# Causal attention: four banks of PSUM for the scores and three for the products for the maxima, in place of three and four

## The reference, cut to what matters

```python
c_q = x @ W_dq
Q = (c_q @ W_uq).reshape(Bx, Sx, N_HEADS, D_K)
c_kv = x @ W_dkv
K = (c_kv @ W_uk).reshape(Bx, Sx, N_HEADS, D_K)
V = (c_kv @ W_uv).reshape(Bx, Sx, N_HEADS, D_K)
scores = jnp.einsum('bqhd,bkhd->bhqk', Q, K) / math.sqrt(D_K)
causal = jnp.tril(jnp.ones((Sx, Sx), dtype=bool))
scores = jnp.where(causal, scores, -jnp.inf)
attn = jax.nn.softmax(scores, axis=-1)
out = jnp.einsum('bhqk,bkhd->bqhd', attn, V).reshape(Bx, Sx, N_HEADS * D_K)
return out @ W_o
```

## Time and profile before

| | us |
|---|---|
| median of 3 runs | 1355.92 |
| lowest, highest | 1352.75, 1357.1 |
| the profiled execution | 1350.49 |
| its span, first to last instruction | 1348.8 |
| TensorE, VectorE, ScalarE, GpSimd busy | 1224.4, 1120.5, 923.6, 745.1 |

### The profile page before, as it was taken

One profiled execution on the slowest core, in us unless ns is written; L12 is line 12 of the kernel. 1 busy time (PEld: TensorE's weight loads), 2 busy tenths in 40 slices (PEclk: granted clock), 3 DMA queues, 4 the chain that ended last, 5 costly groups with the idle time before them and its releaser, 6 DMA issues. The chain is left out here.

```text
span 1348.8 us, 30203 instructions
## 1 busy us (share of the span) xinstructions
PE 1224.4 (91%) x10501; PEld 705.0 (52%) x10501; DVE 1120.5 (83%) x2928; ACT 923.6 (68%) x2463; POOL 745.1 (55%) x753
## 2 busy tenths in 40 slices
PE   4589999999999999888899999799899999997895
PEld 2323434434443443356566666565466666665663
DVE  5788998898999888689899999766599999997675
ACT  4516776777787677678888888433588888885344
POOL 1111212332331233478999999532699999997244
PEclk9859999999999999999999999899999999998998
DMA  4432121112112101011111111100112111111001
GB/s 106 130 107 75 45 59 46 61 51 64 39 39 58 46 15 35 26 40 41 34 30 34 33 33 33 41 0 1 24 32 48 33 33 33 31 27 25 1 17 47
DMA packets 35486, 56.46 MB, mean 42 GB/s; under 512 B 6898, under 2 KB 22652, under 8 KB 33020
## 3 DMA queue, kind: packets, MB, share of 16 engines
q1 hardware_dynamic: 34760, 54.39, 15.3%
q10 hardware_dynamic: 576, 0.15, 0.0%
HBM read 27.78 MB, written 8.39 MB: 27 GB/s over the span
## 5 line engine op out<-in xcount | busy, mean ns | idle before, releaser
L1128 ACT ACTIVATE a_prob<-a_psE 128x512 f32<-128x512 f32 (+1 forms) x608 | 303.0, 591 | 132.1 <-PE a_psE L741 130.6
L1527 DVE CUSTOM_DVE_ANT_0 a_psM<-a_psM,mask_q 128x384 f32<-128x384 f32 (+3 forms) x512 | 234.3, 521 | 32.2 <-PE a_psM L725 31.4
L1360 POOL TENSOR_SCALAR_AFFINE_SELECT a_prob<-a_prob 128x512 f32<-128x512 f32 x128 | 81.1, 641 | 310.0 <-ACT a_prob L1128 306.2
L741 PE MATMUL a_psE<-a_qs,a_ks 84*128 84x512 bf16 (+3 forms) x768 | 238.1, 333 | 12.9 <-ACT a_prob L1128 6.3
L725 PE MATMUL a_psM<-a_ks,a_qs 72*128 72x512 bf16 (+3 forms) x768 | 241.8, 343 | 7.3 <-PEq L106 3.2
L1419 POOL TENSOR_TENSOR w_rn<-w_ssm,mhalf 128x16 f32<-128x16 f32 x64 | 220.5, 3445 | 49.0 <-DVE w_ssm L1619 33.7
L1238 ACT ACTIVATE w_prob<-w_psS,w_bias 128x128 f32<-128x128 f32 x512 | 180.4, 378 | 21.1 <-DVE w_bias L1645 21.1
L1404 POOL TENSOR_TENSOR w_t<-w_raw,w_sin 128x256 f32<-128x256 f32 x252 | 176.6, 734 | 0.0
L1529 DVE TENSOR_REDUCE a_nm<-a_psM 128x1 f32<-128x512 f32 x256 | 158.7, 680 | 15.1 <-PE a_psM L725 13.8
L1409 POOL TENSOR_TENSOR w_rot<-w_t,w_t 128x1024 f32<-128x1024 f32 x63 | 148.7, 2360 | 8.7 <-issue 0.4
L741 PEld LDWEIGHTS a_psE<-a_qs,a_ks 84*128 84x128 bf16 x768 | 74.3, 98 | 148.3 <-ACT a_prob L1128 76.1
(11 more groups left out here) (189 smaller groups left out, 2383.7 us busy)
## 6 DMA issues: line engine op xcount, KB each, us to landing
a_qs<-q_parts SPq DMA_DIRECT2D x16, 576.0 KB
a_ks<-k_parts SPq DMA_DIRECT2D x16, 576.0 KB
q_parts<-p_parts SPq DMA_DIRECT2D x24, 128.0 KB
k_parts<-p_parts SPq DMA_DIRECT2D x24, 128.0 KB
w_vb__707<-w_v__691 SPq DMA_DIRECT2D x16, 128.0 KB, 2.2
w_vb__708<-w_v__691 SPq DMA_DIRECT2D x16, 128.0 KB, 2.3
w_vb__708<-w_v__692 SPq DMA_DIRECT2D x16, 128.0 KB, 2.2
w_vb__709<-w_v__692 SPq DMA_DIRECT2D x16, 128.0 KB, 2.4
```

The costliest lines, as they stand in the source:

```text
L741: mm = pe.matmul(psE[:, r % NRING, j % share * w:(j % share + 1) * w], ks[0:KROWS, g, j, kt * P:(kt + 1) * P], qs[0:KROWS, g, j, q0:q0 + w ...
L1128: act.activation(prob[G % NPROB][:, j - share + 1:j + 1, 0:w], psE[:, r % NRING, 0:share * w].rearrange("p (j n) -> p j n", j=share), ACT. ...
L1527: d = dve.tensor_tensor_reduce(scores, scores, sb["mask_q"][:, 512 - n:512], -1.0, -3.0 * NEG, ALU.add, ALU.min, low)
```

## The change

The rings are re-cut: `psM` has 3 banks, `psE` 4. A product for a maximum then waits for the reader of slot r - 3, a score for the reader of slot r - 4. Since `w_psV` now lies over the first bank of `psE`, from the last stage's first slots on (`E_NARROW`) the scores rotate through the other three banks, and `project_v(0)` waits until that first bank was read. The order of instructions on all five engines is the same as before, and so is the work of each.

```diff
+E_NARROW = E_SLOT["s", LAST_G - 11, 0] // 4 * 4
 def m_bank(r):
-    return r % 4 if r < M_TAIL else 2
+    return r % 3 if r < M_TAIL else 2
+def e_bank(r):
+    return r % 4 if r < E_NARROW else 1 + (r - E_NARROW) % 3
+def e_ring(r):
+    return 4 if r < E_NARROW else 3
...
-        NPROB, NRING, MRING = 5, 3, 4
+        NPROB, MRING = 5, 3
...
-            psE = banks.enter_context(nc.psum_tensor("a_psE", [P, NRING, 512], F32))
+            psE = banks.enter_context(nc.psum_tensor("a_psE", [P, 4, 512], F32))
...
-                    ge(pe, e_read, r - NRING + 1)
-                mm = pe.matmul(psE[:, r % NRING, j % share * w:(j % share + 1) * w], ks[0:KROWS, g, j, kt * P:(kt + 1) * P], qs[0:KROWS, g, j, q0:q0 + w],
+                    ge(pe, e_read, r - e_ring(r) + 1)
+                mm = pe.matmul(psE[:, e_bank(r), j % share * w:(j % share + 1) * w], ks[0:KROWS, g, j, kt * P:(kt + 1) * P], qs[0:KROWS, g, j, q0:q0 + w],
...
                 if G == LAST_G - 9:
+                    pe.wait_ge(e_read, E_NARROW - 3)
                     project_v(0)
```

More of the change, by code:

```diff
@@ L765, in turn_maxima @@
                 pe.wait_ge(nm_parts, 2 * s + half + 1)
-                ge(pe, e_read, r - NRING + 1)
+                ge(pe, e_read, r - e_ring(r) + 1)
                 for t in range(4):
                     i = 4 * half + t
-                    mm = pe.transpose(psEb[0:NM, r % NRING, t * P:(t + 1) * P], nmp[:, s % 2, i, :, :].rearrange("p j a -> p (j a)"), sb["ident_b"])
+                    mm = pe.transpose(psEb[0:NM, e_bank(r), t * P:(t + 1) * P], nmp[:, s % 2, i, :, :].rearrange("p j a -> p (j a)"), sb["ident_b"])
                 mm.then_inc(e_ready, 1)
@@ L791, in turn_o @@
                     r = E_SLOT["t", b, h]
-                    ge(pe, e_read, r - NRING + 1)
-                    out, done = psE[:, r % NRING, :], e_ready
+                    ge(pe, e_read, r - e_ring(r) + 1)
+                    out, done = psE[:, e_bank(r), :], e_ready
                 for t in range(4):
@@ L1127, in exps @@
                         act.wait_ge(e_ready, r + 1)
-                        act.activation(prob[G % NPROB][:, j - share + 1:j + 1, 0:w], psE[:, r % NRING, 0:share * w].rearrange("p (j n) -> p j n", j=share),
+                        act.activation(prob[G % NPROB][:, j - share + 1:j + 1, 0:w], psE[:, e_bank(r), 0:share * w].rearrange("p (j n) -> p j n", j=share),
                                        ACT.Exp, scale=SCALE0).then_inc(e_read, 1)
@@ L1134, in copy_maxima @@
                 ge(act, nm_in[half], 16 * (s - 1))
-                act.activation(nmT[:, s % 2, 512 * half:512 * half + 512], psEb[0:NM, r % NRING, 0:512], ACT.Copy).then_inc(e_read, 1)
+                act.activation(nmT[:, s % 2, 512 * half:512 * half + 512], psEb[0:NM, e_bank(r), 0:512], ACT.Copy).then_inc(e_read, 1)
             def copy_outputs(e, qc):
@@ L1154, in copy_turned @@
                 act.wait_ge(e_ready, r + 1)
-                act.activation(to, psE[:, r % NRING, :], ACT.Copy).then_inc(e_read, 1)
+                act.activation(to, psE[:, e_bank(r), :], ACT.Copy).then_inc(e_read, 1)
             def copy_projected(b, h):
```

## The result

| | before | after |
|---|---|---|
| median (4 runs each) | 1354.34 us | 1370.47 us |
| lowest, highest | 1350.84, 1357.1 | 1368.34, 1371.1 |
| the profiled execution | 1350.49 | 1370.99 |
| its span | 1348.8 | 1369.3 |

The ratio is 1.0118, with a 95% interval of 1.01 to 1.0135. The change costs 16 us by the medians and 20.5 us between the two profiled spans. The two figures fit together: the profiled execution of before lay 3.85 us under its median, that of after 0.5 us above.

What follows compares the result with a forecast made beforehand. VectorE was taken to bound the attention stages, its gaps all at bursts. Eleven stages at 1.78 us (19.6) plus 2.4 for four others gave 22 us, 1378 on the median, stated as 1377, range 1367 to 1387.

Steps and rivals of the forecast that it cites:

- VectorE is the engine to look at: Causal attention stages: VectorE works 25.92 of 28.40 us, ScalarE 20.89, so whatever lengthens VectorE's gaps lengthens the stage.
- The last slot of a segment waits for the reader of r - 3: TensorE's last load for VectorE before each burst waits for one later read; together 1.78 us a stage.
- C: Segment of a stage: turned output 0.43 us late, taken up by shorter waits for ScalarE; charged 0, bounds 0.43 and -0.1.
- B: Segment of a stage: last load moves from 307.65 to 308.24, nothing hides it; charged 0.60 us.
- D: Segment of a stage: turned output 0.53 us late, VectorE's gap of 1.80 us at the burst grows by 0.53.
- E: Segment of a stage: last load 0.65 us late, VectorE's gap of 0.54 us at the burst grows by that.
- A: Segment of a stage: last load 0.09 us late, behind work that VectorE still has; nothing charged.
- The fourth bank of `psE` gives back C's 0.43 and nothing else: Scores may start one exponential (0.50 us) sooner, but products for maxima stay pinned to VectorE; real gain in one segment only.
- A ring of three does not break VectorE's work inside segments: Rival expected the break: one slot a stage 0.5 us late, 14 us more, 1391; chance 0.14.
- The four stages charged at a third: The very first stage and three of some 31.20 us: a third of 1.78 us each, 4 x 0.6 = 2.4.
- The new wait and the narrow ring cost nothing: Last stage: scores keep three banks, and its values already wait for the exponentials asked for; no gain, no loss.
- the clock stays: Attention stages after the first keep 2.4 GHz; the rival, clock falling in two stages, up to 30 us, 1407, chance 0.02.

Runs made afterwards that it cites:

- m3e3: Kernel before with three banks of `psM` in place of four, `psE` kept at three, one bank left empty: 1375.29 us, ratio 1.0175.
- m2e4: Kernel after with two banks of `psM` in place of three, `psE` kept at four, one bank left empty: 1452.72 us, ratio 1.075.
- m5e2: Kernel before with five banks of `psM` in place of four and two of `psE` in place of three: 1414.33 us, ratio 1.0447.
- short_m4e3: Kernel before with VectorE reading only part of each product for its maximum, four banks of `psM`, three of `psE`: 1348.80 us, ratio 0.9975.
- one_m4e3: Kernel before with values of one group after nearly every group, taken a group later (`AV_LAG` 3): 1366.09 us, ratio 1.0093.

## Why the prediction was right, point by point

- **VectorE is the engine to look at, and TensorE's program is what feeds it.** Right: its busy time is unchanged, its waits grew by 20.1 us and the span by 20.5.
- **The last slot of a segment waits for the reader of r - 3.** Right, to 0.07 us or better, though in C two more slots come behind the output. In B the second of four reductions from 317.09 ends at 317.09 + 0.60 + 0.68 = 318.37, and the load comes at 318.42, with the 0.05 of lag that the prediction took from before. In C and D the outputs, forecast 1.28 + 0.05 behind the start of the reductions (321.23 and 330.57), so at 322.56 and 331.90, are loaded at 322.63 and 331.97; the profile calls the end of that wait "issue", so that here it is the time that speaks for the reader and not the name. In E the load comes at 338.62, 0.11 behind a read that ends at 338.51 (it began at 337.78 and took 0.73).
- **The sizes.** B 0.52 (0.60 forecast), C 0.06 (0), D 0.52 (0.53), E 0.65 (0.65), A no gap: 1.75 where 1.78 stood. Only B is a little less: from the late load to VectorE's next read it took 2.88 us before (307.65 to 310.53) and 2.81 after (318.42 to 321.23).
- **The fourth bank of `psE` gives back C's 0.43 and nothing else.** Right in kind: with it C's gap is 0.41, without it 0.70, in the other segments of that stage it changes nothing. It is worth 0.29 us there, and C would have lost 0.35 without it, not 0.43. In the three stages of some 31 us it also gives back 0.2 behind A, which the prediction had at nothing.
- **A ring of three does not break VectorE's work inside segments.** Right: no idle time of VectorE between bursts in the stage shown, and in the fourteen others only one of 0.31 us, which before has too. With two banks it does.
- **The four stages charged at a third.** Wrong in each, right in the sum by luck. From first score to first score the three of some 31 us lost nothing, the first lost 2.2 us (its clock went from 0.78 to 0.75): 2.1 us in all, where 2.4 stood. The reason given, that VectorE is still busy in the three when TensorE comes back, does not hold: in the stage from 330.01 its idle time grew from 3.54 to 4.64 us. What fell is the work that it did inside the stage's edges (27.31 to 26.70 in the windows shown), and the loss comes out in the next stage, which took 29.04 us before and takes 30.79. The two together lost 1.7 us, where 0.6 + 1.78 stood. The other eleven grew by 16.3 us, 1.5 on the mean, in place of 19.6: eight by 1.5 to 1.8, two by 1.1 and 1.2, the last by 0.5. The burst of E just ahead of those two opens no gap in either kernel. That eleven are like the one walked through is the term that was mis-sized, by 3 us.
- **The new wait and the narrow ring cost nothing; the clock stays.** No wait of theirs is seen. But a part of the span was left over, 20.5 against 18.4 for the fifteen stages, and 1.6 to 1.7 us of it is the clock, at a place that the forecast had not looked at (below). By luck it covers half of the 3 us that the stages fell short. That the clock stays was so in the fourteen stages behind the first, all at 1.00, and not in the last one. The windowed layers are as before: from the end of that place to the end of the span it is 1348.8 - 570.0 = 778.8 and 1369.3 - 590.2 = 779.1 us.
- **The median.** 22 us on the span were forecast, 20.5 came; 1377 on the median, 1370.5 came. Most of the difference is that the profiled execution of before was one of its fastest, so that the medians lie 16 us apart; another 1.6 us is that the fourth run of before took its median from 1355.92 to 1354.34.

## What to carry to other kernels

When one in-order engine feeds two rings, a sum of waits does not tell which ring is short: the fourth bank of `psE` took the scores' waits for its readers from 69 us (m3e3) to 13 (after) and gave 5 us, and the bank taken from VectorE's ring cost 23. Look instead at which ring is full when the feeder turns to something long, count one read of that ring's consumer for a bank given or taken (it held here for the fourth bank of `psM`, and fell far short where a ring was cut to two), and check the relief of one ring against the other before counting it, since both can be nearly full at once. And before cutting a stretch that starves a consumer, ask what it costs to leave and enter it once more: here cutting moved the idle time and did not remove it.

## What the runs showed that was not expected

In the burst behind the last group of the last stage, where no maxima are left and the change has no effect on the order, TensorE's clock fell. The stretch ahead of this burst and the burst itself (columns of the earlier trace rows), then the row of its 24 products in the order of time, both before:

```profile
562.00:566.70 4.70, 2.90 (x25) 1.13 (x17) 4.03 (x11) 2.30 (x6) 0.64 (x1) 1.00 0.00 0
566.70:570.00 3.30, 3.22 (x29) 1.26 (x30) 0.91 (x1) 1.40 (x3) 2.81 (x3) 1.00 0.02 5
```

```profile
567.34 2.57 PE L757 MATMUL psO<-a_prob,v_all 128*32 128x512 f32 x24
```

And after:

```profile
580.50:585.20 4.70, 2.93 (x25) 1.16 (x17) 4.03 (x11) 2.27 (x6) 0.63 (x1) 1.00 0.00 0
585.20:590.20 5.00, 4.89 (x29) 1.59 (x30) 0.94 (x1) 1.54 (x3) 4.38 (x3) 0.66 0.00 0
```

```profile
586.09 3.98 PE L770 MATMUL psO<-a_prob,v_all 128*32 128x512 f32 x24
```

Ahead of the burst TensorE does the same in both, 2.9 us of work in 4.7. Before, the granted clock stays at 1.00; after, it is 0.66 on the mean of the burst, that is the lower level of 1.2 GHz for part of it, and the same products take 3.98 us in place of 2.57. In m3e3 this burst took 4.04 us, so it does not go with the fourth bank of `psE`. In m2e4, whose last stage is later, it is

```profile
669.03 4.27 PE L770 MATMUL psO<-a_prob,v_all 128*32 128x512 f32 x24
```

With the shorter reads it took 2.57 us with four banks of `psM` and 4.27 with three, in m5e2 2.57. So of the kernels with these bursts all four with three or two banks of `psM` show it, and none of the three with four or five. That is one trace of each, and how the ring of the maxima comes to matter there stays open; it costs under 2 us here. With other cuts the clock also fell inside the attention stages, as told at short_m4e3, m2e4, one_m4e3 and m5e2; a time of these kernels holds several microseconds of it.
